# Decoder layer with two expert groups: combining both groups' results of a batch at one point, instead of one group at a time

## What is computed

```python
def _moe_group(x2, router_w, wg, wu, wd, top_k):      # 32 experts, hidden 128, top_k 2
    scores = softmax(x2 @ router_w)
    expert_weights, expert_indices = top_k(scores, top_k)
    # every token goes to its two experts
    ys = (silu(xs @ wg[e]) * (xs @ wu[e])) @ wd[e]
    return sum over the token's two experts of expert_weights * ys

out0 = _moe_group(x2, router_w0, wg0, wu0, wd0, 2)
out1 = _moe_group(x2, router_w1, wg1, wu1, wd1, 2)
x3 = layernorm(x2 + (out0 * 2 + out1 * 2) / 4)
```

## Time and profile before

| | us |
|---|---|
| median of 3 runs | 4889.1 |
| lowest, highest | 4886.68, 4891.63 |
| the profiled execution | 4894.84 |
| its span in the profile | 4893.1 |

### The profile page before, as it was taken

One profiled execution on the slowest core, in us unless ns is written; L12 is line 12 of the kernel. 1 busy time (PEld: TensorE's weight loads), 2 busy tenths in 40 slices (PEclk: granted clock), 3 DMA queues, 4 the chain that ended last, 5 costly groups with the idle time before them and its releaser, 6 DMA issues. The chain is left out here.

```text
span 4893.1 us, 133371 instructions
## 1 busy us (share of the span) xinstructions
PE 4755.2 (97%) x38848; PEld 3976.5 (81%) x38848; DVE 3782.2 (77%) x18828; ACT 3412.7 (70%) x13380; POOL 2712.7 (55%) x3750
## 2 busy tenths in 40 slices
PE   7999999999999999999999999999995999999998
PEld 6888888888888888888888888888874766676665
DVE  4888888888888888888888888888883455547777
ACT  5788888878878888887887888788783444444443
POOL 3455555555555555555555555555554555556666
PEclk9999999999999999999999999999997999999999
DMA  4121111112112111211211211121125799878888
GB/s 137 62 69 61 58 65 64 57 60 69 58 58 67 62 58 64 65 58 57 67 62 57 67 64 58 61 67 58 58 78 162 255 299 298 273 246 270 273 273 255
DMA packets 477157, 556.18 MB, mean 114 GB/s; under 512 B 55602, under 2 KB 407860, under 8 KB 475956
## 3 DMA queue, kind: packets, MB, share of 16 engines
q1 hardware_dynamic: 350516, 300.08, 19.9%
q0 software_dynamic: 52224, 146.87, 8.0%
q10 hardware_dynamic: 73728, 100.70, 6.8%
HBM read 270.08 MB, written 277.35 MB: 112 GB/s over the span
## 5 line engine op out<-in xcount | busy, mean ns | idle before, releaser
L527 POOL TENSOR_TENSOR yTl<-yT,yTh 128x256 fp32r<-128x256 f32 x512 | 381.7, 745 | 910.7 <-DVE yTh L979 907.6
L756 ACT ACTIVATE prob<-prob,negmax 128x128 f32<-128x128 f32 x2048 | 799.0, 395 | 102.5 <-DVE negmax L827 98.3
L1155 POOL DMA_INDIRECT y_d<-y,to x576 | 593.2, 1030 | 464.6 <-DVE y L1290 447.8
L756 ACT ACTIVATE xprob<-xprob,xnegmax 128x128 f32<-128x128 f32 x2048 | 792.9, 392 | 1.6 <-DVE xnegmax L827 1.6
L1208 PE MATMUL bank<-moe,xgT 128*128 x2304 | 594.6, 381 | 0.0
L589 POOL DMA_INDIRECT xs_d<-xrow,place x512 | 515.9, 1008 | 128.1 <-issue 128.1
L1290 DVE COPY y<-bank 128x256 f32<-128x256 f32 x576 | 244.5, 424 | 407.4 <-PE bank L1224 290.0
L827 DVE CUSTOM_DVE_ANT_0 prob<-bank,causal 128x128 f32<-128x128 f32 x2048 | 471.7, 286 | 34.0 <-PE bank L695 20.9
L774 ACT COPY probT<-bank 128x512 f32<-128x512 f32 x512 | 300.0, 586 | 248.0 <-PE bank L705 181.1
L827 DVE CUSTOM_DVE_ANT_0 xprob<-bank,xmask 128x128 f32<-128x128 f32 x2048 | 470.5, 286 | 1.2 <-remote 1.2
L837 DVE TENSOR_TENSOR prob<-prob,inv 128x512 f32<-128x512 f32 x512 | 438.9, 857 | 20.2
(11 more groups left out here) (180 smaller groups left out, 14188.3 us busy)
## 6 DMA issues: line engine op xcount, KB each, us to landing
xg<-xs_d SPq DMA_DIRECT2D x576, 136.0 KB
xs_d<-blank SPq DMA_DIRECT2D x248, 272.0 KB
rows<-y_d ACTq DMA_DIRECT2D x256, 256.0 KB
xT_s<-xT SPq DMA_DIRECT2D x128, 128.0 KB
x<-x SPq DMA_DIRECT2D x128, 128.0 KB, 2.0
cT<-cT SPq DMA_DIRECT2D x128, 128.0 KB
x_d<-x SPq DMA_DIRECT2D x128, 128.0 KB, 2.0
sums<-x_d ACTq DMA_DIRECT2D x128, 128.0 KB
```

The costliest lines, as they stand in the source:

```text
L527: nc.gpsimd.tensor_tensor(yT_p[1][:, c, :], yT[:, c, :], yT_p[0][:, c, :].bitcast(F32), ALU.subtract).then_inc(y_split, 1)
L756: last = nc.scalar.activation(dst[:, h, :], dst[:, h, :], ACT.Exp, bias=src_bias[:, h:h + 1], scale=-1.0, accum_out=acc[:, h:h + 1])
L1155: nc.gpsimd.indirect_dma_start(y_d[:, :], bass.IndirectOffsetOnAxis(ap=to[:, m % NTO:m % NTO + 1].bitcast(U32), axis=0), y_s[q][:, :], Non ...
```

## The change

Group 0 is no longer combined while its tiles run. `combined` knows only group 1's points (from step 288 + 42 on, every second step), and k is the batch. At such a point ACT loads `sums` from `x2_d` and then all four rows of each token in one transfer (`rows` is now 128 x 4 x 256, 4 KB per token, 512 KB). VectorE adds four rows: j = 0 and j = 1 where the two additions were, j = 2 behind `h` of the same step, j = 3 behind `h` of the next step, directly ahead of the statistics. Each addition waits for the one before it on `part_ready`. `acc_d`, its stores and its loads are gone. Buffers: `NX` from 10 to 8, `NR` from 4 to 3, `NS` from 8 to 6.

```diff
-    acc_d = nc.dram_tensor("acc_d", (N, D), F32).ap()
...
-            NQ, NX, NTO, NR, NS = 4, 10, 8, 4, 8
+            NQ, NX, NTO, NR, NS = 4, 8, 8, 3, 6
...
-            rows = sb("rows", [P, NR, TOPK, D])
+            rows = sb("rows", [P, NR, SLOTS, D])
...
             def combined(n, group=None):
-                for g in range(NGRP):
-                    b, odd = divmod(n - g * TILES - FIRST, 2)
-                    if not odd and 0 <= b < NB and group in (None, g):
-                        return g, b, g * NB + b
-                return None
+                b, odd = divmod(n - TILES - FIRST, 2)
+                return (1, b, b) if not odd and 0 <= b < NB else None
...
-                            if g:
-                                sp.wait_ge(out_ready, b + 1)
-                                sp.dma_start(out[b, :, :], sums[p][:, :]).then_inc(stored[p], 16)
-                            else:
-                                sp.wait_ge(sum_ready, k + 1)
-                                sp.dma_start(acc_d[b * P:(b + 1) * P, :], sums[p][:, :]).then_inc(stored[p], 16)
+                            sp.wait_ge(out_ready, b + 1)
+                            sp.dma_start(out[b, :, :], sums[p][:, :]).then_inc(stored[p], 16)
...
                             wait(act, stored[k % NS], k // NS * 16)
-                            act.dma_start(sums[k % NS][:, :], (x2_d, acc_d)[g][b * P:(b + 1) * P, :]).then_inc(sums_in[k % NS], 16)
+                            act.dma_start(sums[k % NS][:, :], x2_d[b * P:(b + 1) * P, :]).then_inc(sums_in[k % NS], 16)
                             wait(act, sum_ready, k - NR + 1)
...
                             act.dma_start(rows[:, k % NR, :, :].rearrange("p j d -> p (j d)"),
-                                          y_of_token[b * P:(b + 1) * P, g * TOPK * D:(g + 1) * TOPK * D]).then_inc(rows_in[k % NR], 16)
+                                          y_of_token[b * P:(b + 1) * P, :]).then_inc(rows_in[k % NR], 16)
...
+                    def add(b, k, j):
+                        s = sums[k % NS]
+                        wait(dve, part_ready, (SLOTS - 1) * k + j)
+                        done = v.scalar_tensor_tensor(s[:, :], rows[:, k % NR, j, :], weight[:, b, j:j + 1], s[:, :], ALU.mult, ALU.add)
+                        done.then_inc(sum_ready if j == SLOTS - 1 else part_ready, 1)
...
-                            v.scalar_tensor_tensor(s[:, :], rows[:, k % NR, 0, :], weight_of(g, b, 0), s[:, :], ALU.mult, ALU.add).then_inc(part_ready, 1)
+                            add(b, k, 0)
                         if t.live(3):
...
                             v.tensor_copy(y_s[q][:, :], YB[q % 2][:, 0:D]).then_inc(y_in, 1)
                         if now:
-                            dve.wait_ge(part_ready, k + 1)
-                            v.scalar_tensor_tensor(s[:, :], rows[:, k % NR, 1, :], weight_of(g, b, 1), s[:, :], ALU.mult, ALU.add).then_inc(sum_ready, 1)
+                            add(b, k, 1)
                         if t.live(1):
...
                         full = combined(n - COMBINE - 1, 1)
+                        if now:
+                            add(now[1], now[2], 2)
                         if full:
                             g, b, k = full
+                            add(b, k, 3)
                             dve.wait_ge(sum_ready, k + 1)
                             v.bn_stats(stat[:, :], sums[k % NS][:, :]).then_inc(stat_step, 1)
```

More of the change, by code:

```diff
@@ L1135, in _ @@
                     for p in range(NS):
-                        sp.wait_ge(stored[p], 16 * (NGRP * NB // NS))
+                        sp.wait_ge(stored[p], 16 * ((NB + NS - 1 - p) // NS))
                 @block.gpsimd
@@ L1273, in _ @@
                     dve.wait_ge(spare_ready, 2)
-                    def weight_of(g, b, j):
-                        return weight[:, b, g * TOPK + j:g * TOPK + j + 1]
+                    def add(b, k, j):
[3 more added lines that the diff above has]
+                        done.then_inc(sum_ready if j == SLOTS - 1 else part_ready, 1)
                     def iteration(t, n):
```

## The result

The changed kernel takes 4922.93 us (median of 4 runs, 4917.44 to 4926.46), the kernel before 4890.36 (4 runs); the ratio is 1.0065 with a 95% interval of 1.005 to 1.008. It is 33 us slower. The forecast was about 3 us and 4892, in a range that ended at 4922. The spans of the two profiled executions are 4921.4 and 4893.1, 28.3 apart.

A forecast was written before the change was run, and what follows sets the result against it. The expert stage was taken as bound by the PE round plus VectorE additions on its path, not VectorE's total. -45.8 + 43.5 + 5.5 = +3.2 us gave 4898.0 profiled, 4892 us as median; range 4874 to 4922.

The forecast's parts named there:

- Part 1: Group 0 without combining: tiles fall from 1.959 to 1.780 us as L1293 leaves the path before h, -45.8 us.
- Part 2: Group 1 with four additions: even step 2.08 us, odd step 2.20, 0.354 more per pair over 123 batches, +43.5 us.
- Queues and buffers: ACT issues, rows with three slots, xg with eight buffers and DMA time per pair: all covered, cost nothing.
- rival 2: ACT waits for the store before a buffer of sums is free: +17 us, 4909 us, chance 0.08.
- Rival 1: Group 1: DMA engines become the bound once a pair's DMA time exceeds 4.02 us; +26 us, 4918 us, chance 0.15.
- Rival 3: Group 1: each addition costs its full duration and blocks the next; +53 us, 4945 us, chance 0.03.
- Rivals 4 and 5: Group 1's j = 3 partly hides, 4876 us, chance 0.15; group 0 keeps 1.96 us, 4938 us, chance 0.03.
- The tail: Last five batches, VectorE back to back with two more additions each, 2.9 us apart, loads ending before it: +5.5 us.

The follow-up runs named there:

- the run with the one edit to the kernel before: Kernel before, with only the second addition (L1293) moved behind h in both groups: 4803.91 us, 0.982 times before.
- the seven buffers: Changed kernel with seven buffers of sums instead of six, seven of xg, store lag 15: 4922.15 us, 1.0059 times before.
- the half rows: Changed kernel loading only the first two of four rows per token, used for all four additions: 4915.63 us.
- all three edits: Changed kernel with seven buffers of sums, scaling ahead of the fourth addition, second addition behind h: 4847.09 us, 0.9912 times before.
- the run with the scaling first: Changed kernel with the scaling (L1317) moved ahead of the fourth addition in the same VectorE step: 4901.11 us, 1.0016 times before.
- With two additions only: Changed kernel still loading four rows per token, additions j = 2 and j = 3 taken out: 4870.94 us, 0.9964 times before.

## Why the prediction was right or wrong

The parts of the sum, in us:

| | forecast | profiled |
|---|---|---|
| group 0 without combining | -45.8 | -44.5 (tiles 40 to 300: 509.0 to 464.5) |
| group 1 with four additions | +43.5 | +71.4 (tiles 330 to 575: 480.4 to 551.8) |
| tail | +5.5 | +6.6 (15.0 to 21.6) |
| before the first tile | 0 | -5.5 (3764.1 to 3758.6) |
| sum | +3.2 | +28.0 |

- **Part 1 was right**, in size and in cause: the run with the one edit to the kernel before shows that the place of L1293 was what group 0's combining cost.
- **Part 2 failed in one term**: "statistics 0.33, scaling 0.32". The scaling's pitch was read where it began 0.23 us into a scatter; with the fourth addition ahead it begins at 0.75 and is followed after 0.54 in 87 batches. That is worth 19 us, by 544.0 against 525.0. With the scaling moved, the group runs at 2.146 us per tile and the odd step at 2.20, which are the forecast's figures, so the price of the additions was right. The even step was right too.
- **Queues and buffers**: the forecast discussed `rows` and xg, and put the queues into the sum at nothing; the six buffers of `sums` stand only in rival 2, "when a store needs more than about 5 us", with 0.08. That rival was true and is the smaller term: 8 us in the changed kernel, by the seven buffers and by the half rows alike. Both of its sizes were off. A store has 3.5 us before its buffer is wanted, not 4.3, and needs 4.3 in the median, up to 6.1. Its chance was too low: the chain had shown a DMA of 5.71 us, and the forecast itself raised the load.
- **Rival 1** is refuted. Group 1 was faster at 0.95 and 0.99 share than at 0.91. The load matters through the latency of a store, not as a rate. The DMA time of a pair came to 0.91 x 4.50 = 4.10 us, past the 4.02 that was to decide, and yet the group ran faster when only the order changed; with all three edits the same bytes took 0.99 x 3.88 = 3.84. (The larger `rows` moved at 3.18 us per MB for their queue, 46.3% for 29.14 MB, and not at the scatter's 2.63 that the forecast took.)
- **Rival 3** is refuted by the even step and by the 2.20 of the run with the scaling first.
- **Rivals 4 and 5** did not occur: the odd step hid nothing, and group 0 gave its cost back.
- **The tail** came out near the forecast and in the main for its reason, with little to spare. The batches are 2.9 to 3.2 us apart, where 2.9 was forecast, and VectorE waits for loads for 0.3 us in all:

```profile
4905.09 0.40 DVE L1317 TENSOR_SCALAR sums<-sums,mv,rstd 128x256 f32<-128x256 f32 x1
...
4907.98 0.40 DVE L1317 TENSOR_SCALAR sums<-sums,mv,rstd 128x256 f32<-128x256 f32 x1
...
4908.62 1.53 DVE L1271 SCALAR_TENSOR_TENSOR sums<-rows,weight,sums 128x256 f32<-128x256 f32 x3 [0.25 <-DMA rows<-y_d]
...
4911.20 0.40 DVE L1317 TENSOR_SCALAR sums<-sums,mv,rstd 128x256 f32<-128x256 f32 x1
```

  The loads end just behind VectorE, where the forecast had them end before it. With two additions only the tail was 19.9 us (last copy of y at 4848.7, span 4868.6), nearly as long, and there it is the loads: two of `rows` stand in its chain of waits with 4.95 and 6.13 us, one of them behind a store's buffer.

The two terms missed, 19 and 8 us, are the 28 us by which group 1 exceeded its forecast, but for one. The steps of the changed kernel add up the same way: over the 2.20 us of an undisturbed odd step, the 87 with a collision have 17 us too much and the 36 without one 12, the waits among them. The range left out the sum of the two terms because each unknown was bounded by rows in which the neighbours in time on another engine were the old ones. One slip changes nothing: rival 4 was priced at 4876, and the range names it with 4874.

## What to carry to other kernels

Before taking work off the list or gathering it in one place, ask where each piece stands in the in-order queue: an addition ahead of the value that the next engine waits for cost its full 0.40 us in each pair of tiles, and the same addition behind it next to nothing, in both groups. A duration read from a trace belongs to an instruction and to its moment; when the order changes, look at what the other engines do at the new moment. An edit that moves an operation also moves what waits for it, so one run may hold two effects. And when buffers are traded for larger transfers, count the steps between the release and the next use against the slowest transfer seen, not the median.

## What was not expected of the hardware

- A one-input scaling of VectorE (128 x 256) takes 0.62 us and GpSimd's scatter instruction 1.28 us when the one starts 0.75 us into the other, against 0.40 and 0.96 to 1.04. The scaling takes 0.60 to 0.65 us for starts from 0.48 to 0.77 us into the scatter's instruction (332 of 344), and 0.40 or 0.41 for all 403 up to 0.44 us and all 41 from 0.78 us on. The same operation with two tensor inputs stays at 0.47 us, while the scatter still takes 1.28.
- The transfers kept 343 GB/s at a share of 0.99 over 200 us, in 42107 packets of which 32247 are under 2 KB, in a stage that ran at 1.94 us per tile where 1.98 was expected (all three edits).
